# Flamingo block on one core: residual transposed by token tiles inside the last out tile, router ahead of the last routes, six query copies on ScalarE

## The chip, the cores and the metric

One NeuronCore of a Trainium2 chip runs the whole program in one launch. The metric is the device time of the program in microseconds (us), taken as the median of several runs. TensorE (PE in the profile) does matmuls and transposes into PSUM, ScalarE (ACT) and VectorE (DVE) read PSUM and write SBUF, GpSimd (POOL) works on SBUF alone, and SyncE (SP) issues DMAs. Each engine executes its own list of instructions in order and waits on semaphores for the others.

## The reference, cut to what matters

```python
# x: 4 x 1024 x 256, ctx: 4 x 154 x 256, 16 heads of 16
x = x + tanh(g_xattn) * xattn(layernorm(x), ctx, ctx)        # xpos rotation on q and k, softmax over 154 keys
x = x + tanh(g_ffn) * ffn(layernorm(x))

def mole(x, W, b, A, Bm, Rw):                                # three LoRA experts of rank 8
    gates = softmax(x @ Rw)                                  # 3 gates for each token
    z = einsum('bsd,edr->ebsr', x, A)                        # 24 values for each token
    return x @ W + b + 1/8 * einsum('ebsr,erh->bsh', z * gates, Bm)
def ffn(x):
    return mole(relu(mole(x, W1, b1, A1, B1, R1)), W2, b2, A2, B2, R2)     # 256 -> 1024 -> 256
```

## The kernel before, in words

The 4 x 1024 tokens are cut into eight chunks of 512 tokens (c = 0 to 7), each of four token tiles of 128 (k = 0 to 3). The kernel is a pipeline of eight steps written out by hand, one for each chunk, and one epilogue. Step c does the attention of chunk c, the second layernorm, the router and the hidden layer of chunk d = c - 1, and the output layer (the "out tiles") of chunk e = c - 2. So step 0 has attention alone, step 1 ("second") has no out tiles, and steps 2 to 7 ("full") have all three. Each engine has its own function `step` with its own order, and the semaphores (`Count`, with `at(n, k)` for the k-th signal of step n) tie the orders together. Nothing plans the order at build time: it is the order of the lines.

Most matmuls run in fp32r on operands split in a high and a low part: three products instead of one. So each operand on its way from PSUM is copied once (the high part) and subtracted once (the low part).

The stretch that the change touches lies in the middle of a step, in this order on TensorE (its `step` begins at L1178):

- out tile 3 of chunk e (`out_tile(e, 3)`, L1112): 8 hidden tiles x 3 products into bank 0 of `psF`; its last 28 columns are the second router's and the LoRA values (z2).
- `transpose_x(d, ...)` (L943): eight 128 x 128 transposes of the normalised residual `xn` of chunk d into two banks of `psX`, feature half f = 0 first with its four token tiles, then f = 1. It waits until all four tiles of `xn` are written by ScalarE (L411).
- `q_transposes` for g = 0 and 1 (L1085): the rotated queries of chunk c, four transposes for each of eight groups g, into bank g % 4 of `psX`.
- `lora2_operand(e, 1)` (L1122): transposes of the gated LoRA values `zs` of out tiles 2 and 3.
- `router1(d)` (L1028): the first router and LoRA values (z1) of chunk d, which need the high and the low part of the transposed residual (`xT_hi`, `xT_lo`).
- `out_lora(e, 1)` (L1128), then `q_transposes` for g = 2 to 7, with the two halves of the first hidden tile (`hidden_main(d, 0)`, L1052) behind g = 3 and g = 5, and `lora1_operand(d)` (L1037).
- Then a loop of 16 `max_scores` (L1099), each with half a hidden tile; VectorE reduces each one (L733) and writes the low half of each hidden tile (L726).

On ScalarE (`step` at L455) the same stretch is: `normalise` (four tiles of `xn`), the exponential of the second router's gates for tiles 2 and 3 (`gate2_exp(e, 1)`, L440), `x2T_high` (the high part, two copies, L356), then the copies of the queries of g = 0, 2, 4, 6 into `qT` (L356); behind the first of them stand `gate2_copy(e, 1)` and `gate1_exp(d)`.

On VectorE: statistics of the first layernorm of chunk c + 1 (L574, L579), `copy_z2(e, 3)` (L740), `gates2(e, 1)` (L590 to L614: maximum, shift, exponential by ScalarE, sum, reciprocal, weights, gated values, and their split into `zs`), `x2T_low(d)` (the low part, L639), the query copy of g = 1 (L721), `gates1_shift(d)` (L783, L590, L592), g = 3, `gates1_weigh(d)` (L598 to L614), `finish(e, 2)` (L751), g = 5, `finish(e, 3)`, g = 7, and the loop of reductions.

`max_scores(0)` of TensorE waits until six of the eight query groups are copied (L1093 to L1095), three by either engine, and `max_scores(1)` for all.

Of the kernel before, what the change touches and what calls it, by code (L numbers as in the profile page):

```python
# [65 lines left out]
def build(nc, x, ctx_in, wq, wkv, wo, w1, w2, a1, lora, tables, out):  # L66
    with ExitStack() as stack:
# [121 lines left out]
        qT_ps, qT_a, qT_v = count("qT_ps", NG), count("qT_a", NG // 2), count("qT_v", NG // 2)  # L189
# [164 lines left out]
        def _(act):  # L354
# [100 lines left out]
            def step(b, u, first=False, second=False, last=False):  # L455
# [22 lines left out]
                if full:  # L478
                    gate2_exp(e, 1)
# [3 lines left out]
                for g in range(0, NG, 2):  # L483
                    act.wait_ge(qT_ps.sem, qT_ps.at(c, g + 1))
                    copy(qT[0:KS, g, :], psX[0:KS, g % 4, :]).then_inc(qT_a.sem, 1)
                    if full and g == 0:
                        gate2_copy(e, 1)
                    if not first and g == 0:
                        gate1_exp(d)
# [79 lines left out]
        def _(dve):  # L569
# [25 lines left out]
            def gates_weigh(v, e, n, i, K, e_done):  # L595
# [15 lines left out]
                V.tensor_copy(zs[:, K, 0:NL], zg[:, K])  # L611
                V.tensor_copy(zs[:, K, 64:64 + NL], zg[:, K]).then_inc(v.sem, 1)
# [181 lines left out]
            def step(b, u, first=False, second=False, last=False):  # L794
# [31 lines left out]
                if not last and not first:  # L826
                    ln1_stats(c + 1)
                if full:
                    copy_z2(e, 3)
                    gates2(e, 1)  # L830
                if not first:
                    x2T_low(d)
                q_transposed(c, 1)
                if not first:
                    gates1_shift(d)
                q_transposed(c, 3)
# [4 lines left out]
                q_transposed(c, 5)  # L841
                if full:
                    finish(e, u, 3)
                q_transposed(c, 7)
# [86 lines left out]
        def _(pe):  # L931
# [6 lines left out]
            def transpose_x(c, banks, src_s, ps):  # L938

                pe.wait_ge(src_s.sem, src_s.at(c))  # L940
                for f in range(FT):
                    for k in range(TT):
                        ins = nc.tensor.transpose(banks[:, f, tokens(k)], xn[:, k, P * f:P * f + P], ident)  # L943
                    ins.then_inc(ps.sem, 1)

# [126 lines left out]
            def q_transposes(c, g, first):  # L1072

                if g == 0:
                    pe.wait_ge(q_lo.sem, q_lo.at(c))
                    pe.wait_ge(q_hi2.sem, q_hi2.at(c))
                elif g == 2 and not first:
                    pe.wait_ge(x2T_hi_s.sem, x2T_hi_s.at(c - 1))
                    pe.wait_ge(x2T_lo_s.sem, x2T_lo_s.at(c - 1))
                elif g >= 4 and g % 2 == 0:  # L1080
                    pe.wait_ge(qT_a.sem, qT_a.at(c, g // 2 - 1))
                elif g >= 4:
                    pe.wait_ge(qT_v.sem, qT_v.at(c, g // 2 - 1))
                for k in range(TT):
                    ins = nc.tensor.transpose(psX[0:KS, g % 4, tokens(k)].bitcast(F32R), qs[:, k, g, :], ident_r[:, :])  # L1085
                ins.then_inc(qT_ps.sem, 1)

            def max_scores(c, i):
# [3 lines left out]
                if i < 2:  # L1092
                    n = 3 if i == 0 else 4  # L1093
                    pe.wait_ge(qT_a.sem, qT_a.at(c, n))
                    pe.wait_ge(qT_v.sem, qT_v.at(c, n))  # L1095
# [7 lines left out]
            def out_tile(d, k, m0=0, m1=HT):  # L1103
# [4 lines left out]
                if k == 3:  # L1108
# [69 lines left out]
            def step(b, u, first=False, second=False, last=False):  # L1178
# [23 lines left out]
                if full:  # L1202
# [4 lines left out]
                    out_tile(e, 3)  # L1207
                if not first:
                    transpose_x(d, psX[:, 2:4, :], ln2_out, x2T_ps)
# [3 lines left out]
                for g in range(2):  # L1213
# [3 lines left out]
                if not first:  # L1217
                    router1(d, second)
                if full:
                    out_lora(e, 1)  # L1220
                for g in range(2, NG):
                    q_transposes(c, g, first)
                    if not first and g in (3, 5):
                        hidden_main(d, 0, second, (g // 2 - 1,))
# [83 lines left out]
LAST = B * UB - 1  # L1308
F_OF_K = [0, 1, 2, 0]
# [71 lines left out]
```

## Time and profile before

| | us |
|---|---|
| median of 3 runs | 604.42 |
| lowest, highest | 602.23, 604.69 |
| the profiled execution, its own time | 603.83 |
| span of the profiled execution, first to last instruction | 602.0 |
| busy in it: PE, DVE, ACT, POOL | 524.9, 416.3, 238.3, 84.9 |

The time of an execution is 1.8 us longer than the span of its profile. The rows further down are read in a few views: the page (busy times and chain shares), the waits (who waited for whom), the chain of waits (followed back from the last instruction, at each step to what released it), the timeline of one engine, the groups of instructions, and windows (busy times and the granted clock of a stretch). An instruction is named by its line, what it writes and what it reads: `DVE L639 ... xT_lo<-psX,xT_hi` is the low part of the transposed residual. In a timeline `x2` means two instructions merged into one row, and `[0.61 <-DVE zs L614]` that the engine had been idle for 0.61 us until that instruction released it. The full steps repeat one another closely; the step shown is that of c = 5, at 340 to 406 us.

### The profile page before, as it was taken

The numbers are of one execution on the slowest core, as the hardware profiler recorded it, in microseconds if no ns is written. First come the engines' busy times: TensorE is split into PE (matmuls) and PEld (weight loads), VectorE is DVE, ScalarE is ACT, GpSimd is POOL, SyncE is SP. The second block draws the span as 40 slices with busy tenths as digits, with TensorE's granted clock in tenths as the row PEclk, the third lists the DMA queues.
The fourth block names the chain that finished last, engine by engine and source line by source line (L and its number), as shares of the span: only waits on it lengthen the run. The fifth ranks groups of instructions, "written<-read, shape, count | busy, mean of one in ns | idle before, by whom it ended". The sixth has DMA issues, their size and how long they took to land.

```text
span 602.0 us, 8537 instructions
## 1 busy us (share of the span) xinstructions
PE 524.9 (87%) x3360; PEld 400.0 (66%) x3360; DVE 416.3 (69%) x960; ACT 238.3 (40%) x389; POOL 84.9 (14%) x121
## 2 busy tenths in 40 slices
PE   2668864999989998999989998999899999989795
PEld 1545454855977487856976497738885697649574
DVE  4667355867989478958888488867896578644423
ACT  3252514363354624454335424452436343442210
POOL 2426012011110112011201121011201110101000
PEclk9865975999999999999999999999999999999798
DMA  7301010010101000011002010101002000200000
GB/s 265 112 2 36 2 35 2 0 49 1 37 0 44 31 35 2 37 48 35 1 1 73 1 35 1 66 19 36 1 4 70 0 2 1 73 1 1 2 35 36
DMA packets 6132, 18.50 MB, mean 31 GB/s; under 512 B 932, under 2 KB 1772, under 8 KB 5964
## 3 DMA queue, kind: packets, MB, share of 16 engines
q10 hardware_dynamic: 4005, 12.53, 6.0%
q1 hardware_dynamic: 2087, 5.42, 2.7%
q8 instruction: 27, 0.44, 0.3%
q14 instruction: 13, 0.11, 0.1%
HBM read 13.49 MB, written 4.19 MB: 29 GB/s over the span
## 4 chain that ended last, share of the span: by engine, by line
PE 71%; DVE 16%; ACT 8%; issue 3%; POOL 1%; DMA 1%; ACTq 0%; DVEq 0%
PE psF L1112 17%; PE psF L1052 11%; PE psX L1099 6%; ACT probs L521 4%; PE psX L988 4%; PE psX L1158 4%; PE psX L970 4%; DVE max_t L733 4%; PE psO L1172 3%; PE psF L1172 3%; PE psF L1175 3%; PE psO L1175 3%; PE psF L1058 2%; PE psX L1085 2%; DVE h_lo L726 2%
## 5 line engine op out<-in xcount | busy, mean ns | idle before, releaser
L733 DVE TENSOR_REDUCE max_t<-psX 128x4 fp32r<-128x616 f32 x128 | 99.8, 795 | 6.0 <-PE psX L1099 3.0
L521 ACT ACTIVATE probs<-psX 128x1024 f32<-128x1024 f32 x64 | 63.8, 1024 | 50.5 <-PE psX L1158 50.5
L1112 PE MATMUL psF<-w_hi,h_hi 128*128 128x284 f32 x256 | 76.8, 300 | 2.4 <-DVE h_lo L726 1.5
L1112 PE MATMUL psF<-w_lo,h_hi 128*128 128x284 f32 x256 | 75.2, 294 | 0.0
L1112 PE MATMUL psF<-w_hi,h_lo 128*128 128x284 f32 x256 | 74.9, 293 | 0.0
L1099 PE MATMUL psX<-km,qT 96*128 96x308 f32 x256 | 65.2, 341 | 7.1 <-DVE max_t L733 3.6
L1099 PEld LDWEIGHTS psX<-km,qT 96*128 96x128 f32 x256 | 48.7, 204 | 23.8 <-DVE max_t L733 12.1
L431 ACT ACTIVATE h_hi<-psF 128x512 fp32r<-128x512 f32 x64 | 37.3, 594 | 63.0 <-PE psF L1058 63.0
L726 DVE SCALAR_TENSOR_TENSOR h_lo<-psF,h_hi 128x512 fp32r<-128x512 f32 x64 | 43.7, 685 | 15.7 <-ACT h_hi L431 15.7
L1112 PEld LDWEIGHTS psF<-w_hi,h_hi 128*128 128x128 f32 x256 | 48.2, 188 | 7.8 <-issue 4.6
L311 POOL TENSOR_TENSOR x<-x,tab 128x256 f32<-128x256 f32 x32 | 22.3, 730 | 206.3 <-DMA x<-in_x_dram 206.3
L1052 PE MATMUL psF<-xT_lo,w_hi 128*128 128x512 f32 x128 | 51.4, 412 | 0.0
L1158 PE MATMUL psX<-qT,km 98*128 98x512 f32 x128 | 44.8, 445 | 4.3 <-ACT probs L521 4.0
L1112 PEld LDWEIGHTS psF<-w_hi,h_lo 128*128 128x128 f32 x256 | 48.3, 188 | 0.0
L1112 PEld LDWEIGHTS psF<-w_lo,h_hi 128*128 128x128 f32 x256 | 48.2, 188 | 0.0
L1052 PE MATMUL psF<-xT_hi,w_hi 128*128 128x512 f32 x128 | 42.3, 412 | 1.0 <-DVE zc L783 1.0
L1158 PEld LDWEIGHTS psX<-qT,km 98*128 98x128 f32 x128 | 20.5, 195 | 32.3 <-issue 15.5
L1052 PE MATMUL psF<-xT_hi,w_lo 128*128 128x512 f32 x128 | 40.9, 401 | 0.0
L757 DVE STREAM_TRANSPOSE heads_t<-psF 128x512 f32<-128x512 f32 x16 | 11.5, 717 | 34.7 <-PE psF L1175 34.7
L323 POOL TENSOR_TENSOR probs<-probs,tab 128x1024 f32<-128x1024 f32 x8 | 19.0, 2370 | 106.0 <-DVE probs L646 106.0
L1085 PE MATMUL psX<-ident_r,split 128*96 128x128 f32 x256 | 24.7, 250 | 4.9 <-DVE split L678 4.9
L1085 PEld LDWEIGHTS psX<-ident_r,split 128*96 128x96 f32 x256 | 22.9, 133 | 8.1 <-issue 6.0
(155 smaller groups left out, 990.2 us busy)
## 6 DMA issues: line engine op xcount, KB each, us to landing
x<-in_x_dram ACTq DMA_DIRECT2D x8, 512.0 KB, 3.3
x_ln<-in_x_dram ACTq DMA_DIRECT2D x7, 512.0 KB, 3.3
out_dram<-x ACTq DMA_DIRECT2D x7, 512.0 KB, 2.6
heads_t<-in_w_dram SPq DMA_DIRECT2D x1, 1024.0 KB, 8.5
heads_t<-in_w_dram SPq DMA_DIRECT2D x1, 994.0 KB, 4.6
tab<-in_tables_dram SPq DMA_DIRECT2D x1, 674.0 KB, 7.0
x_ln<-in_x_dram SPq DMA_DIRECT2D x1, 512.0 KB, 3.4
wkv_sb<-in_wkv_dram SPq DMA_DIRECT2D x1, 512.0 KB, 9.8
```

The source lines that it names most:

```text
L431: nc.scalar.activation(h_hi[:, m, :], psF[:, (m + 1) % 3, :], ACT.Relu).then_inc(w1_hi_s.sem, 1)
L521: nc.scalar.activation(dst, psX[:, 2 * (i % 2):2 * (i % 2) + 2, :], ACT.Exp).then_inc(sc_exp.sem, 1)
L726: V.scalar_tensor_tensor(out=h_lo[:, m, :], in0=psF[:, (m + 1) % 3, :], scalar=0.0, in1=h_hi[:, m, :].bitcast(F32), op0=ALU.max, op1=ALU.s ...
L733: V.tensor_reduce(max_t[:, k, half, :].rearrange("p (h g) -> p g h", h=2)[:, 2 * j:2 * j + 2, :], psX[:, 2 * j:2 * j + 2, 0:2 * S].rearran ...
L970: ins = mm(o_ps, a[:, f, tokens(k)], w[:, f, :], start=n == 0, stop=n == 5)
L1052: mm(psF[:, (m + 1) % 3, :], w[:, f, P * m:P * m + P], a[:, f, :], start=n == 0, stop=False)
L1085: ins = nc.tensor.transpose(psX[0:KS, g % 4, tokens(k)].bitcast(F32R), qs[:, k, g, :], ident_r[:, :])
L1099: ins = mm(psX[:, g % 4, 0:2 * S], qT[0:KS, g, tokens(k)], km[0:KS, g, :, :].rearrange("p h s -> p (h s)"), start=True, stop=True)
L1112: ins = mm(psF[:, F_OF_K[k], 0:W2N], a[:, m, tokens(k)], w[:, m, :], start=m == 0 and i == 0, stop=m == HT - 1 and i == 2)
L1158: ins = mm(o_ps, km[:, n // 2, j, 0:P], qT[:, n // 2, :], start=True, stop=True)
L1172: mm(pv_bank(g), vr_sb[:, g, :], probs_r[:, g, :], start=True, stop=False)
L1175: ins = mm(pv_bank(g)[32 * j:32 * j + 32, :], v_sb[:, h, :], probs[:, h % 8, :], start=False, stop=True)
```

## The change: what it does

- TensorE's out tile 3 is cut in two: six of its eight hidden tiles (18 matmuls), then the transposes of `xn`, then the last two hidden tiles (6 matmuls). The new `transpose_x2` goes by token tiles: for each k it waits for that tile of `xn` alone and transposes both feature halves.
- `router1(d)` stands directly behind the query groups 0 and 1. Groups 2 to 5 follow, then `lora2_operand(e, 1)`, the first half of hidden tile 0, `out_lora(e, 1)`, groups 6 and 7, the second half of hidden tile 0, `lora1_operand(d)`.
- ScalarE copies the query groups 0, 1, 2, 3, 4, 6 and VectorE 5 and 7 (before: four each). `gate2_exp(e, 1)` moves from ahead of `x2T_high` to behind group 1; `gate2_copy(e, 1)` and `gate1_exp(d)` from behind group 0 to behind group 3.
- VectorE does `x2T_low(d)` ahead of `copy_z2(e, 3)` and `gates2(e, 1)`, and `gates1_shift`, group 5, `gates1_weigh`, `finish(2)`, group 7, `finish(3)` behind them.
- The two copies of the gated values into `zs` (its columns 0 and 64 on) become one instruction with the input read twice.
- The waits follow: a group g of 4 or more waits for copy g - 3 of ScalarE; `max_scores(0)` for five copies of ScalarE and one of VectorE. The epilogue keeps its order, and has the one copy into `zs`.

```diff
@@ -186,7 +186,7 @@
         q_ps, q_evac = count("q_ps", 2), count("q_evac", 2)
         q_cos, q_sin, q_rot = count("q_cos", 1), count("q_sin", TT), count("q_rot", 1)
         q_hi, q_hi2, q_lo = count("q_hi", 1), count("q_hi2", 1), count("q_lo", 1)
-        qT_ps, qT_a, qT_v = count("qT_ps", NG), count("qT_a", NG // 2), count("qT_v", NG // 2)
+        qT_ps, qT_a, qT_v = count("qT_ps", NG), count("qT_a", 6), count("qT_v", 2)
...
@@ -475,17 +475,17 @@
                          q_rc.rearrange("p k (g r) -> p (k g) r", r=32)).then_inc(done.sem, 1)
                 if not first:
                     normalise(1, x1[:, 1 - u], d, ln2_rstd, ln2_out, (xT_ps, c))
-                if full:
-                    gate2_exp(e, 1)
                 if not first:
                     x2T_high(d)
 
-                for g in range(0, NG, 2):
+                for g in QT_ACT:
                     act.wait_ge(qT_ps.sem, qT_ps.at(c, g + 1))
                     copy(qT[0:KS, g, :], psX[0:KS, g % 4, :]).then_inc(qT_a.sem, 1)
-                    if full and g == 0:
+                    if full and g == 1:
+                        gate2_exp(e, 1)
+                    if full and g == 3:
                         gate2_copy(e, 1)
-                    if not first and g == 0:
+                    if not first and g == 3:
                         gate1_exp(d)
                 if not first:
                     gate1_copy(d)
@@ -608,8 +608,8 @@
                                 zw[:, K].unsqueeze(3).to_broadcast([P, nk, NE, R]),
                                 ALU.mult).then_inc(v.sem, 1)
                 dve.wait_ge(v.sem, v.at(n, i + 6))
-                V.tensor_copy(zs[:, K, 0:NL], zg[:, K])
-                V.tensor_copy(zs[:, K, 64:64 + NL], zg[:, K]).then_inc(v.sem, 1)
+                V.tensor_copy(zs[:, K].rearrange("p k (t r) -> p k t r", r=32)[:, :, 0::2, 0:NL],
+                              zg[:, K].unsqueeze(2).to_broadcast([P, nk, 2, NL])).then_inc(v.sem, 1)
                 dve.wait_ge(v.sem, v.at(n, i + 7))
                 V.tensor_tensor(zs[:, K, 32:32 + NL], zg[:, K], zs[:, K, 0:NL].bitcast(F32),
                                 ALU.subtract).then_inc(v.sem, 1)
@@ -825,23 +825,21 @@
                     copy_z2(e, 2)
                 if not last and not first:
                     ln1_stats(c + 1)
+                if not first:
+                    x2T_low(d)
                 if full:
                     copy_z2(e, 3)
                     gates2(e, 1)
                 if not first:
-                    x2T_low(d)
-                q_transposed(c, 1)
-                if not first:
                     gates1_shift(d)
-                q_transposed(c, 3)
+                q_transposed(c, 5)
                 if not first:
                     gates1_weigh(d)
                 if full:
                     finish(e, u, 2)
-                q_transposed(c, 5)
+                q_transposed(c, 7)
                 if full:
                     finish(e, u, 3)
-                q_transposed(c, 7)
                 for i in range(16):
                     reduce_max(c, i)
                     if first and i == 5:
@@ -943,6 +941,15 @@
                         ins = nc.tensor.transpose(banks[:, f, tokens(k)], xn[:, k, P * f:P * f + P], ident)
                     ins.then_inc(ps.sem, 1)
 
+            def transpose_x2(d):
+
+                for k in range(TT):
+                    pe.wait_ge(ln2_out.sem, ln2_out.at(d, k + 1))
+                    for f in range(FT):
+                        ins = nc.tensor.transpose(psX[:, 2 + f, tokens(k)], xn[:, k, P * f:P * f + P], ident)
+                        if k == TT - 1:
+                            ins.then_inc(x2T_ps.sem, 1)
+
             def ctx_transposed(b, src):
 
                 pe.wait_ge(ctx_loaded.sem, ctx_loaded.at(b))
@@ -1077,10 +1084,8 @@
                 elif g == 2 and not first:
                     pe.wait_ge(x2T_hi_s.sem, x2T_hi_s.at(c - 1))
                     pe.wait_ge(x2T_lo_s.sem, x2T_lo_s.at(c - 1))
-                elif g >= 4 and g % 2 == 0:
-                    pe.wait_ge(qT_a.sem, qT_a.at(c, g // 2 - 1))
                 elif g >= 4:
-                    pe.wait_ge(qT_v.sem, qT_v.at(c, g // 2 - 1))
+                    pe.wait_ge(qT_a.sem, qT_a.at(c, g - 3))
                 for k in range(TT):
                     ins = nc.tensor.transpose(psX[0:KS, g % 4, tokens(k)].bitcast(F32R), qs[:, k, g, :], ident_r[:, :])
                 ins.then_inc(qT_ps.sem, 1)
@@ -1090,9 +1095,8 @@
 
                 half, k, j = i // 8, i % 8 // 2, i % 2
                 if i < 2:
-                    n = 3 if i == 0 else 4
-                    pe.wait_ge(qT_a.sem, qT_a.at(c, n))
-                    pe.wait_ge(qT_v.sem, qT_v.at(c, n))
+                    pe.wait_ge(qT_a.sem, qT_a.at(c, 5 + i))
+                    pe.wait_ge(qT_v.sem, qT_v.at(c, 1 + i))
                 else:
                     pe.wait_ge(max_red.sem, max_red.at(c, i - 1))
                 for g in range(4 * half + 2 * j, 4 * half + 2 * j + 2):
@@ -1105,7 +1109,7 @@
                 if k == 0:
                     pe.wait_ge(w1_hi_s.sem, w1_hi_s.at(d))
                     pe.wait_ge(w1_lo_s.sem, w1_lo_s.at(d))
-                if k == 3:
+                if k == 3 and m0 == 0:
                     pe.wait_ge(y_out.sem, y_out.at(d, 1))
                 for m in range(m0, m1):
                     for i, (a, w) in enumerate(((h_hi, w2_hi), (h_lo, w2_hi), (h_hi, w2_lo))):
@@ -1204,24 +1208,30 @@
                     out_tile(e, 2, 0, HT // 2)
                     out_lora(e, 0)
                     out_tile(e, 2, HT // 2, HT)
-                    out_tile(e, 3)
-                if not first:
-                    transpose_x(d, psX[:, 2:4, :], ln2_out, x2T_ps)
+                    out_tile(e, 3, 0, HT - 2)
+                if not first:
+                    transpose_x2(d)
                     pe.wait_ge(x1_s.sem, x1_s.at(d))
                 else:
                     pe.wait_ge(q_evac.sem, q_evac.at(c))
-                for g in range(2):
+                if full:
+                    out_tile(e, 3, HT - 2, HT)
+                q_transposes(c, 0, first)
+                q_transposes(c, 1, first)
+                if not first:
+                    router1(d, second)
+                for g in range(2, 6):
                     q_transposes(c, g, first)
                 if full:
                     lora2_operand(e, 1)
                 if not first:
-                    router1(d, second)
+                    hidden_main(d, 0, second, (0,))
                 if full:
                     out_lora(e, 1)
-                for g in range(2, NG):
-                    q_transposes(c, g, first)
-                    if not first and g in (3, 5):
-                        hidden_main(d, 0, second, (g // 2 - 1,))
+                q_transposes(c, 6, first)
+                q_transposes(c, 7, first)
+                if not first:
+                    hidden_main(d, 0, second, (1,))
                 if not first:
                     lora1_operand(d)
                 for i in range(16):
@@ -1306,6 +1316,7 @@
 PV_AFTER = [3, 5, 8, 10]
 PV_SLOT = {3: 0, 5: 1, 8: 2}
 LAST = B * UB - 1
+QT_ACT = [0, 1, 2, 3, 4, 6]
 F_OF_K = [0, 1, 2, 0]
```

## Rows read from the trace of the kernel before

**Rows 1.** The page, part 1: busy us, share of the span, instructions.
```profile
PE 524.9 (87%) x3360; PEld 400.0 (66%) x3360; DVE 416.3 (69%) x960; ACT 238.3 (40%) x389; POOL 84.9 (14%) x121
```
**Rows 2.** The page, part 4: shares of the chain that ended last.
```profile
PE 71%; DVE 16%; ACT 8%; issue 3%; POOL 1%; DMA 1%; ACTq 0%; DVEq 0%
```
**Rows 3.** Waits of PE, whole span: us in total, times, longest.
```profile
PE psO L1122 <- DVE zs L614: 7.3, 8, 2.3
PE psF L1028 <- DVE xT_lo L639: 6.7, 7, 1.0
PE psX L1099 <- DVE qT L721: 2.7, 6, 0.4
```
**Rows 4.** Chain of waits, 338 to 412 us: start us, us, what.
```profile
357.57 4.72 PE psF L1112 x36
...
364.20 0.10 DVE zs L612
...
364.54 1.21 DVE xT_lo L639 x2
...
365.88 1.08 PE psF L1028 x32
...
371.23 0.52 PE psX L1099 x2
```
**Rows 5.** Timeline of PE, 340 to 384 us: start, us, instruction, idle before.
```profile
362.36 1.09 PE L943 MATMUL psX<-ident_r,xn 128*128 128x128 f32 x8
363.21 0.77 PE L1085 MATMUL psX<-ident_r,split 128*96 128x128 f32 x8
364.59 0.34 PE L1122 MATMUL psO<-ident_r,zs 128*96 128x128 f32 x2 [0.61 <-DVE zs L614]
...
370.34 0.45 PE L1037 MATMUL psO<-ident_r,zs 128*96 128x128 f32 x4
```
**Rows 6.** Timeline of ACT, the same stretch.
```profile
360.23 2.08 ACT L411 ACTIVATE xn<-x,ln_b,ln_r 128x256 f32<-128x256 f32 x4 [2.20 <-POOL ln_b L304]
...
363.05 1.08 ACT L356 ACTIVATE xT_hi<-psX 128x512 fp32r<-128x512 f32 x2
```
**Rows 7.** Timeline of DVE, the same stretch.
```profile
362.32 0.19 DVE L740 COPY zc<-psF 128x28 f32<-128x28 f32 x1 [0.36 <-PE psF L1112]
...
367.02 0.32 DVE L783 STREAM_TRANSPOSE zc<-psF 128x128 f32<-128x128 f32 x1 [0.69 <-PE psF L1028]
...
367.97 0.69 DVE L721 CAST qT<-psX 96x512 fp32r<-96x512 f32 x1 [0.23 <-PE psX L1085]
...
370.01 0.48 DVE L751 SCALAR_TENSOR_TENSOR x<-psF,gate,x 128x256 f32<-128x256 f32 x1
...
371.99 0.79 DVE L733 TENSOR_REDUCE max_t<-psX 128x4 fp32r<-128x616 f32 x1
```
**Rows 8.** Groups by form: count | busy us, mean ns | idle before.
```profile
L721 DVE CAST qT<-psX 96x512 fp32r<-96x512 f32 x32 | 21.8, 680 | 4.6 <-PE psX L1085 4.5
L356 ACT ACTIVATE qT<-psX 96x512 fp32r<-96x512 f32 x32 | 18.8, 589 | 16.4 <-PE psX L1085 16.4
...
L611 DVE CAST zs<-zg 128x96 fp32r<-128x96 f32 x8 | 1.7, 211 | 0.3
```
**Rows 9.** Chain of waits, 75 to 125 us, in step c = 1.
```profile
95.32 2.08 ACT xn L411 x4
97.45 1.97 PE psX L943 x8
...
100.88 1.94 PE psF L1028 x32
```
**Rows 10.** Timeline of ACT, 88 to 112 us.
```profile
99.45 0.60 ACT L356 ACTIVATE xT_hi<-psX 128x512 fp32r<-128x512 f32 x1 [0.26 <-PE psX L943]
```
**Rows 11.** Windows: us, busy of each engine, granted clock, DMA share, GB/s.
```profile
105.20:107.20 2.00, 2.00 (x15) 1.71 (x14) 1.41 (x5) 0.59 (x1) 0.00 (x0) 0.60 0.00 0
...
355.00:371.20 16.20, 14.14 (x143) 12.95 (x143) 14.05 (x51) 8.64 (x17) 3.33 (x8) 1.00 0.01 2
```

## The prediction

> **What bounds the kernel now.** The page first: TensorE is busy for 524.9 of 602.0 us [rows 1], and the chain that ended last runs through it for 71%, through VectorE for 16% and ScalarE for 8% [rows 2]. So a change is worth what it takes out of TensorE's idle time on that chain, not what it takes from another engine. The waits come next. In the stretch that the change touches TensorE waits for three things: for the gated LoRA values ahead of the second LoRA operand, for the low part of the transposed residual ahead of the router, and for the last query copies ahead of the first maxima [rows 3]. Of these totals, six full steps carry 0.61, 0.95 and 0.44 us each in the step shown (the other five within 0.2 us of it), 2.0 us together.
>
> The chain through the step of c = 5 tells why. Out tile 3 ends at 362.29, VectorE then works off the second gates until 364.54, only then the low part of the residual until 365.75, then the router starts at 365.88, and the first maxima at 371.23 [rows 4]. The low part could have been made earlier: its input was transposed by 363.45 and copied by ScalarE by 364.13 [rows 5, 6]. VectorE's order holds it back behind the gates, which nobody needs so early. The granted clock is 1.00 here, the 2.4 GHz level [rows 11], so no part of the wait is a slow array.
>
> **The full step, moment by moment.** I lay the new order over the same step with the old durations.
>
> TensorE. One matmul of the out tile takes 4.72/36 = 0.131 us [rows 4], so the 6 that now stand behind take 0.79, and the first 18 end at 361.50. The tiles of the normalised residual end at about 360.8, 361.3, 361.8 and 362.31 [rows 6]. A transpose starts every (363.21 - 362.36)/8 = 0.106 us and takes 0.27 [rows 5]. Token tiles 0 to 2 are done by 362.13; tile 3 starts at 362.36, as the first transpose did before, and its two halves are readable at 362.63 and 362.74 instead of about 362.95 and 363.37. The 6 matmuls follow until 363.37, the query groups 0 and 1 until 363.9.
>
> ScalarE makes the two high parts until 363.73, 0.4 earlier. Its exponential no longer stands in front, which costs nothing here: the copies had to wait 0.1 us for it.
>
> VectorE is idle from 361.96 [rows 7], so the low parts start at 363.26 and, with 0.60 us from one to the next [rows 4], end at 364.54 instead of 365.75: 1.21 earlier. The router starts at 364.69, which leaves TensorE 0.8 us idle ahead of it.
>
> Behind it VectorE has no gap any more, and its list sets the pace:
> - second gates, from 362.32 to 364.54 before = 2.22 [rows 4, 7], now less one copy. The second copy adds 0.10 [rows 4]; the joint one is wider, of which the nearest row is 96 columns in 211 ns [rows 8]. The ends are 0.10 saved and 0.11 lost; I take 0.07 saved: 2.15, to 366.69;
> - transpose of z1, maximum and shift: 367.02 to 367.97 less 0.23 idle = 0.72 [rows 7], to 367.41;
> - copy of query group 5: 0.61, to 368.02;
> - weights and gated values: 367.97 + 0.61 = 368.58 to 370.01 = 1.43 [rows 7], less 0.07: to 369.38;
> - two finishes and one copy: 370.01 to 371.99 held two of each, 1.98 [rows 7]; less one copy, 1.37: the first reduction can start at 370.75 instead of 371.99.
>
> TensorE beside it: router to the first LoRA operand took 370.34 - 365.88 = 4.46 [rows 4, 5]. The second LoRA operand is new in this stretch, 0.34 at most [rows 5]. So it is ready at 364.69 + 4.8 = 369.5, and VectorE's values are there at 369.38 + 0.09 + 0.13 (as from low part to router) = 369.6. The operand takes 0.45, the first maxima start at 370.05: their wait for copies (0.44) is gone, because all but group 7 are copied by 368.6 on ScalarE and 368.1 on VectorE. That is 371.23 - 370.05 = 1.18 on TensorE and 1.24 on VectorE. I take **1.2 us for each of six full steps, 7.2 us**. The loop behind it, in which both engines keep the same lead, has no deadline that isn't set by this start, so nothing takes it back.
>
> The two more copies on ScalarE (589 ns each against 680 on VectorE [rows 8]) are hidden by its 0.5 to 2.4 us gaps. The exponential is wanted at 364.54 + 0.62 = 365.16 (before, 362.32 to 362.94); ScalarE's group 0 can start at 363.8, group 1 ends at 364.9. So its cover is 0.3 us thick. Behind group 3 the gate copy and the router's exponential end at about 367.8, wanted at 368.0: cover 0.2. If either cover is gone, each 0.1 us late costs 0.1 us in each step.
>
> On VectorE's joint copy the page "VectorE: DVE Perf Modes" of the Trainium skill (Mode 2x_2P) bears: a copy within SBUF moves two elements a cycle when the outermost dimension splits evenly over the two read ports, otherwise one. The input here is read twice through a zero stride and the output strided; if that loses the mode, my estimate from the page's 0.96 GHz is 0.05 and 0.10 us longer, and the sum would be 7.7 instead of 8.3 below. No row shows such a copy.
>
> **The other steps.** In step c = 1 there is no out tile. The residual's last tile ends at 97.40, the eight transposes run 97.45 to 99.42, the second high part ends at 100.05, the router starts at 100.88 [rows 9, 10]. The transposes start every 0.20 us here, at half clock, so with tiles 0 to 2 done beforehand the second half of tile 3 is readable at about 98.2 and its high part ends at 99.1; VectorE's two low parts, 0.60 apart behind 98.6, end at 99.9. The router starts at 100.0: 0.9 us gained. Ends: 0.4, if the clock comes back at the same moment as before and the work pulled ahead of it runs at half rate, and 1.3.
>
> The clock there: it reads 0.60 over 105.2 to 107.2 [rows 11], so it went from 1.2 to 2.4 GHz at about 106.8, some 9 us after TensorE began again at 97.45. "TensorE: Matmul & The Clock Gate" (Part 1) of the Trainium skill says that full rate follows sustained activity; by that rule the transposes that start at 96 would bring it forward by up to 1.5 us, and the sum would be about 0.4 higher.
>
> Step c = 0 has no residual. ScalarE's copies in series still keep ahead of TensorE at half clock: nothing. The epilogue keeps its order; two gate chains lie on its path, 0.07 each, with the first gates 0.2.
>
> **Sum.** 7.2 + 0.9 + 0.2 = 8.3 us. Against the profiled execution's 603.83 that is 595.5; the median of the runs is 0.6 above it, which gives 604.42 - 8.3 = **596.1 us**.
>
> **Rivals.**
> - A, as worked out: 596.1, its own range 594.3 to 597.9 (1.0 to 1.35 a step, 0.4 to 1.3 in step 1). Chance 62%.
> - B, the thin covers and TensorE's turns eat half: semaphores and starts that I put at zero add 0.6 us a step to VectorE's list. Every handoff of the new order has under 0.5 us to spare. 6 x 0.6 + 0.6 = 4.2, so 600.2. For it: no gap is left on the list. Against: the old chain shows only 0.02 to 0.15 us at a handoff. 17%.
> - C, the clock comes back early in step 1: half of the 6 us between 100.9 and 106.8 is up to 3 us more, 593.1. Against: the idle time ahead is shortened by 1.5 of 7.6 us only. 8%.
> - D, no change that can be told: ScalarE serves group 2, group 3 and the gate copy (0.59 + 0.59 + 0.38) only after the router's shift at 367.41, so its exponential comes 1.0 us late. 6 x 0.2 + 1.1 = 2.3, 602.1. For it: groups 2 and 3 are transposed behind the router now. Against: they are there 1 us before the shift ends. 8%.
> - E, slower: ScalarE's strict order. The 6 matmuls (0.79), groups 0 and 1 on TensorE (0.55) and their two copies (1.18) stand ahead of the second gates' exponential. If they run behind the low part instead of beside it, the exponential comes at 364.54 + 2.52 = 367.06, 1.9 late: 6 x 0.7 lost against before, less 1.1 elsewhere, 607.5. It decides from 1.4 us late on. Against: they wait for nothing of VectorE. 5%.
>
> **How the numbers follow.** Three runs of the kernel before lie within 2.5 us, so under 0.5%, 3.0 us, can't be told from no change. Faster by more: A, C and most of B, 85%. Within: D and the rest of B, 10%. Slower: E, 5%. The range goes from C's neighbourhood to B, 592.8 to 600.5; it leaves out D, E and the thin ends, under 2 in 10.
>
> **What would show it.** In a full step: no wait of TensorE for the gated values, about 0.8 us for the low part still, 0.2 or less ahead of the first LoRA operand, none for query copies; VectorE without a gap from the low parts to the first reduction; out tile 3 ending 1.1 us later against the last normalised tile, and the first maxima 7.7 instead of 8.9 us behind that tile. The prediction is wrong if VectorE stands waiting for an exponential, if the low parts don't start within 1.0 us of the last normalised tile, or if the step's 1.2 us come back as waits in the loop of reductions.

## The result and the profile after

The changed kernel takes 590.59 us (median of 4 runs, 589.12 to 592.8) against 604.5 us of the kernel before (median of 4, 602.23 to 604.69). The ratio is 0.978, 95% interval 0.976 to 0.980: 13.9 us faster. In a second comparison it took 592.24 us against 604.1 us, 0.979 (0.977 to 0.981). I had said 596.1, with 592.8 to 600.5: right in sign, too small by 5.5 us, and outside the range.

The page of the changed kernel (profiled execution 589.12 us, span 587.3), parts 1 and 4, to lay beside [rows 1] and [rows 2]:

```profile
PE 519.7 (88%) x3360; PEld 394.4 (67%) x3360; DVE 403.1 (69%) x920; ACT 245.9 (42%) x405; POOL 84.8 (14%) x121
...
PE 68%; DVE 15%; ACT 10%; issue 3%; POOL 3%; DMA 1%; ACTq 0%; DVEq 0%
```

GpSimd's share of the chain rose from 1% to 3% and ScalarE's from 8% to 10%: the chain now runs through the second layernorm. The waits of TensorE, to lay beside [rows 3]:

```profile
PE psF L1035 <- DVE xT_lo L639: 5.0, 7, 1.0
...
PE psO L1126 <- DVE zs L614: 3.6, 2, 2.2
```

The wait for the gated values went from eight times to the two of the epilogue, the wait for query copies is gone, and the one for the low part went from 6.7 to 5.0 us. The chain through the full step c = 5, against [rows 4]:

```profile
348.70 0.29 DVE ln_m L579 x3
...
349.53 1.04 POOL ln_r L301
...
350.96 2.08 ACT xn L411 x4
...
353.09 0.34 PE psX L949
...
353.46 0.61 ACT xT_hi L356
...
354.09 1.30 DVE xT_lo L639 x2
...
355.52 1.08 PE psF L1035 x32
356.60 1.24 PE psX L1090 x16
357.85 0.14 PE psO L1126 x2
...
360.28 0.29 PE psO L1044 x4
360.56 0.35 PE psX L1103 x2
```

Before, the chain came through out tile 3 and the second gates; now it goes from the layernorm's statistics over GpSimd's power to the four normalised tiles, one transpose, the high and the low part, the router, and then down TensorE's own list without a break. Both kernels can be read against the end of the last normalised tile, 362.31 before and 353.04 now (starts as in the engines' timelines; the chain counts a matmul from the end of the one ahead and so shows the LoRA operand and the maxima 0.16 us later):

| behind the last normalised tile | before | forecast | measured |
|---|---|---|---|
| low part ends | 3.44 | 2.23 | 2.34 |
| router starts | 3.57 | 2.38 | 2.48 |
| first LoRA operand starts | 8.03 | 7.29 | 7.08 |
| first maxima start | 8.92 | 7.74 | 7.36 |
| first reduction starts | 9.68 | 8.44 | 8.29 |

So the full step gained 1.56 us where I had put 1.2. The timeline of VectorE in the changed kernel (start, us, instruction, idle before) shows one gap from the low part to the first reduction, the 0.27 us in which ScalarE takes the exponential of the second gates. The kernel before had the same 0.27, and it lies inside the 2.22 us that the forecast took for these gates. The rest of the list is without a gap, as forecast:

```profile
354.09 1.29 DVE L639 TENSOR_TENSOR xT_lo<-psX,xT_hi 128x512 fp32r<-128x512 f32 x2 [1.39 <-ACT xT_hi L356]
355.29 0.18 DVE L740 COPY zc<-psF 128x28 f32<-128x28 f32 x1
...
356.14 0.16 DVE L598 TENSOR_REDUCE zsum<-zex 128x2 f32<-128x6 f32 x1 [0.27 <-ACT zex L440]
...
357.22 0.21 DVE L614 TENSOR_TENSOR zs<-zg,zs 128x48 fp32r<-128x48 f32 x1
357.35 0.31 DVE L783 STREAM_TRANSPOSE zc<-psF 128x128 f32<-128x128 f32 x1
...
357.89 0.17 DVE L592 TENSOR_TENSOR zsh<-zc,zmax 128x12 f32<-128x12 f32 x1
357.98 0.68 DVE L721 CAST qT<-psX 96x512 fp32r<-96x512 f32 x1
...
359.48 0.26 DVE L611 CAST zs<-zg 128x192 fp32r<-128x192 f32 x1
359.77 0.26 DVE L614 TENSOR_TENSOR zs<-zg,zs 128x96 fp32r<-128x96 f32 x1
...
361.33 1.63 DVE L733 TENSOR_REDUCE max_t<-psX 128x4 fp32r<-128x616 f32 x2
```

Over the whole span, by the start of the first maxima of steps 1 and 7: 4.6 us came up to step 1 (107.85 to 103.22), 9.3 in the six full steps, 0.7 behind them, 14.7 together. My terms were 0.9, 7.2 and 0.2.

### The profile page after: what moved, and what is told of

Same layout as the page of the kernel before. It is cut to its first block, busy times and chain, and to the rows that moved or that the text cites. A ratio compares the mean times of both kernels' runs of the same rounds, so it can differ in the third digit from the quotient of the medians.

```text
span 587.3 us, 8513 instructions
## 1 busy us (share of the span) xinstructions
PE 519.7 (88%) x3360; PEld 394.4 (67%) x3360; DVE 403.1 (69%) x920; ACT 245.9 (42%) x405; POOL 84.8 (14%) x121
## 4 chain that ended last, share of the span: by engine, by line
PE 68%; DVE 15%; ACT 10%; issue 3%; POOL 3%; DMA 1%; ACTq 0%; DVEq 0%
PE psF L1059 12%; PE psF L1116 11%; PE psX L1103 6%; ACT probs L521 4%; PE psX L977 4%; PE psX L995 4%; PE psX L1162 4%; DVE max_t L733 4%; PE psO L1176 3%; PE psF L1176 3%; PE psF L1179 3%; PE psO L1179 3%; PE psX L1090 3%; ACT xn L411 3%; DVE ln_s L574 2%
## 5 line engine op out<-in xcount | busy, mean ns | idle before, releaser
L521 ACT ACTIVATE probs<-psX 128x1024 f32<-128x1024 f32 x64 | 63.8, 1024 | 49.5 <-PE psX L1162 49.5
L356 ACT ACTIVATE qT<-psX 96x512 fp32r<-96x512 f32 x48 | 26.5, 591 | 15.7 <-PE psX L1090 15.3
L356 ACT ACTIVATE split<-heads_t 128x512 fp32r<-128x512 f32 x16 | 10.0, 626 | 45.1 <-DVE heads_t L772 45.1
```

The source lines that it names most:

```text
L356: return nc.scalar.activation(out_ap, in_ap, ACT.Copy, **kw)
L521: nc.scalar.activation(dst, psX[:, 2 * (i % 2):2 * (i % 2) + 2, :], ACT.Exp).then_inc(sc_exp.sem, 1)
```

## The experiments

Each kernel was timed against the kernel before on the same chip; the median of that kernel is given where it matters. "A full step" below is the change of the distance from the router of step 2 to that of step 7, over five, against the changed kernel's 63.68 us a step. In what was expected, theory S says that VectorE's order bounds the full step, and theory C that part of the gain hangs on TensorE's clock.

**One part undone at a time, on the changed kernel.** VectorE's order:

```diff
-                if not first:
-                    x2T_low(d)
                 if full:
                     copy_z2(e, 3)
                     gates2(e, 1)
+                if not first:
+                    x2T_low(d)
```


> The changed kernel with VectorE's low part of the residual behind the second gates again, all else kept. Theory S (VectorE's order was the bound of the full step): the gates' exponential stands behind ScalarE's group 1 in this order, so the low part ends about 3.0 us later, 6 x 3.0 = 18 us: about 608, router of c = 5 some 5.5 us behind the last normalised tile. Rival (the gain is TensorE's own: transposes inside the out tile): under 1 us a step, below 597.

619.01 us, ratio 1.025 (1.022 to 1.028), 4.2 us a full step. The chain of this kernel in its step c = 5:

```profile
370.72 1.08 ACT qT L356 x2
371.80 0.10 ACT zex L440
...
373.22 1.21 DVE xT_lo L639 x2
...
374.56 1.93 PE psF L1035 x32
376.50 1.65 PE psX L1090 x16
```

The router starts at 374.56, 5.40 behind the last normalised tile (369.16), as theory S said, held by the exponential behind ScalarE's two query copies. The 11 us beyond the forecast are mostly the clock: after TensorE had waited 3.60 us in front of it, the router took 1.93 us instead of 1.08 and the query transposes 1.65 instead of 1.24. It took 1.45 to 1.94 us in five of the six full steps, and 1.08 in one. So the order alone decides some 3 us a step, and the idle time that it makes costs another 1.2 at 1.2 GHz.

**Token tiles.** The out tile whole, the transposes behind all four tiles:

```diff
-                    out_tile(e, 3, 0, HT - 2)
+                    out_tile(e, 3)
...
-                    transpose_x2(d)
+                    transpose_x(d, psX[:, 2:4, :], ln2_out, x2T_ps)
...
-                if full:
-                    out_tile(e, 3, HT - 2, HT)
```


> The changed kernel with out tile 3 whole and the eight transposes behind all four tiles, feature half first, as before. Theory S: out tile 3 ends before the last normalised tile in any case, and only the first half is readable 0.2 to 0.3 us later: 0.25 x 6 + 0.6 in step 1, about 592.7. Rival (token tiles are a main term): 1.2 a step, 598 or more.

595.4 us (before: 603.87), ratio 0.986 (0.983 to 0.989); 0.35 us a full step, where theory S had put 0.25. The time as a whole is 2.7 us above its 592.7. By its profile this kernel is 5.9 us behind the fastest execution of the changed kernel: 2.8 up to the first maxima of step 1, 2.0 in the six full steps and 1.0 behind the first maxima of step 7. Against the slowest execution of the changed kernel it is 0.65 us ahead up to step 1. So the 2 us of the full steps are the token tiles'; the rest is not shown to be, because the clock moves these two stretches from one execution to the next (below).

**Query copies.** Four on each engine:

```diff
-QT_ACT = [0, 1, 2, 3, 4, 6]
+QT_ACT = [0, 2, 4, 6]
...
                     x2T_low(d)
+                q_transposed(c, 1)
...
                     gates1_shift(d)
+                q_transposed(c, 3)
                 q_transposed(c, 5)
```
ScalarE's gate work moves with its list: `gate2_exp(e, 1)` stands behind group 0 here, and `gate2_copy(e, 1)` and `gate1_exp(d)` behind group 2.

> The changed kernel with four query copies on each engine, ScalarE 0, 2, 4, 6 and VectorE 1, 3, 5, 7. Theory S: VectorE has no gap between the low part and the first reduction, so two more copies of 0.6 us put the first maxima 1.15 us later: 6.9 us, about 597.5. Rival (ScalarE's copies are no part of the gain, TensorE's own work is the bound): 591.

599.23 us (before: 603.87), ratio 0.992 (0.989 to 0.995), 1.2 us a full step: theory S, with its 597.5 missed by 1.7 us. Once VectorE's list has no gap, every copy on it is on the path.

**The joint copy into zs**, made two again:

```diff
-                V.tensor_copy(zs[:, K].rearrange("p k (t r) -> p k t r", r=32)[:, :, 0::2, 0:NL],
-                              zg[:, K].unsqueeze(2).to_broadcast([P, nk, 2, NL])).then_inc(v.sem, 1)
+                V.tensor_copy(zs[:, K, 0:NL], zg[:, K])
+                V.tensor_copy(zs[:, K, 64:64 + NL], zg[:, K]).then_inc(v.sem, 1)
```


> The changed kernel with two copies of the gated values into zs instead of one. Theory S: 0.07 and 0.08 us more on VectorE's list in a full step, of which 0.1 reaches TensorE: 0.7 us, 591.3. Rival: nothing.

593.36 us, ratio 0.981 (0.978 to 0.985), which overlaps the changed kernel's interval, so the times can't tell theory S from its rival; in the trace it is 0.14 us a full step. The groups of the changed kernel give the two forms of the joint copy:

```profile
L611 DVE CAST zs<-zg 128x96 fp32r<-128x96 f32 x16 | 3.4, 210 | 0.6
...
L611 DVE CAST zs<-zg 128x192 fp32r<-128x192 f32 x8 | 2.1, 260 | 0.3
```

96 columns more cost 50 ns, about 1.9 elements a nanosecond. "VectorE: DVE Perf Modes" of the Trainium skill gives this mode two results a cycle (Mode 2x_2P) and VectorE a clock of 0.96 GHz (The TRN2 errata). From these figures I estimate 1.92 elements a nanosecond, and the trace agrees: the fast mode is kept with the input read through a zero stride, and the forecast's lower sum for the other case falls away.

**One part alone, on the kernel before.** The orders without token tiles and with four copies each, and the token tiles without the orders (the edits are the parts of the diff above):

> The kernel before with the new orders alone (low part ahead of the second gates, router ahead of the second LoRA operand, gates' exponential behind ScalarE's first copy), but the whole transposes and four copies on each engine. If the parts add: 1.55 gained in the full step, less 0.3 for the tiles and 1.15 for the copies, 0.1 a step: about 603.5. Rival (the orders are the whole gain): 595.

604.27 us against 603.75, ratio 1.001 (1.000 to 1.002). No change, as the sum of the parts said. The chain shows what took the wait's place, VectorE's list with the copies on it:

```profile
362.80 1.29 DVE xT_lo L639 x2
364.09 0.59 DVE qT L721
...
367.43 1.20 DVE qT L721 x2
...
370.12 0.48 PE psO L1037 x4
370.60 0.35 PE psX L1099 x2
```

> The kernel before with the transposes by token tiles inside out tile 3 alone. The gates of tiles 2 and 3 wait for the out tile, which now ends 1.1 us later, and the low part stands behind them: 0.9 us later in each of six full steps, 0.9 gained in step 1: 608.5. Rival (early transposes help by themselves): 600.

616.47 us, ratio 1.021 (1.019 to 1.023): slower, and by more than I had put. Its chain:

```profile
367.04 0.80 PE psF L1121 x6
...
367.87 0.20 DVE zc L740
...
370.08 1.21 DVE xT_lo L639 x2
...
371.43 1.93 PE psF L1037 x32
```

The six matmuls stand in front of the gates, the gates in front of the low part. TensorE's wait for the gated values grew from 0.61 to 1.77 us, the clock read 0.81 over 368 to 372 and 0.50 over 372 to 376, and the router ran at half rate. So neither half of the change is worth anything alone: they come to 0 and +13 us, and the whole, with the query copies moved as well, to -12 to -14.

**The clock.** First the spread of the changed kernel:

> The changed kernel as it is, for its spread. Theory C (some 3 to 4 us of the gain hang on when the clock returns in step 1 and the epilogue): runs at about 589 and about 592, in step with the mean granted clock of 0.958 and 0.951. Rival: one time, whatever the clock.

Five runs: 589.56 us at a mean granted clock of 0.958, 591.23 at 0.954, 592.24 and 592.98 at 0.951, 593.14 at 0.949. The time follows the clock. The kernel before does so more loosely: of 14 runs in this comparison the fastest, 602.82, had 0.950 and the slowest, 606.24, had 0.942, but at 0.945 alone they go from 603.19 to 605.53. The profiled execution of the changed kernel was one of its fastest. Step 1 in it (first fence) and in the profiled execution of this second comparison (second fence), chains of waits:

```profile
83.74 4.61 PE psX L995 x24
...
98.43 1.08 PE psF L1035 x32
99.51 1.26 PE psX L1090 x16
```
```profile
84.87 5.47 PE psX L995 x24
...
100.43 1.94 PE psF L1035 x32
102.36 1.87 PE psX L1090 x16
```

The same instructions of the same program, at 2.4 GHz in the one and at 1.2 in the other. In the second the first maxima of step 1 come at 106.7, which is 1.1 us before the kernel before's 107.85; in the first at 103.22, 3.5 us earlier still.

Much of that lies ahead of the stretch whose order was changed. The first line of each fence is the output projection of step 1. In the kernel before it is

```profile
84.46 5.45 PE psX L988 x24
```

The last normalised tile of step 1, which follows from it, ends at 97.40 in the kernel before, at 95.85 in the first execution and at 97.84 in the second. Behind that tile the router comes after 3.48 us before, and after 2.58 and 2.59 in the changed kernel: 0.9 us gained in both, as forecast, and this is the order. The first maxima come after 10.45, 7.37 and 8.86 us. So of the 4.6 us of the profiled execution 1.55 came ahead of the tile, where the projection started 0.72 us earlier and took 0.84 less; 0.9 is the order; and 2.2 came behind the router, with the router itself at 2.4 GHz and not at 1.2.

Then the kernel was run with TensorE kept busy, and the kernel before likewise:

```diff
+            def busy(bank, n):
+                for _ in range(n):
+                    mm(bank, ident, wkv_sb[:, 0, :], start=True, stop=True)
...
+                if second:
+                    busy(psX[:, 3, :], 10)
                 if not first:
                     project_out(d, c, second)
+                if second:
+                    busy(psX[:, 3, :], 12)
```


> The kernel before, with 10 dummy matmuls (128x512, f32) into a free PSUM bank ahead of the output projection of step 1 and 12 behind it, so that TensorE does not idle there. Theory C: the clock stays at 2.4 GHz through step 1, which takes 2.6 us from the projection and 3 to 4 from the rest of the step: about 598.5. Rival (the clock is no part of it): 604.5 or later.

> The changed kernel with the same dummy matmuls. Theory C: 1.7 us from the projection and 1 to 2 from the rest, 586 to 587, and every run at one time. The difference to the kernel before with the same dummies is then the order alone: 9.3 for six full steps and 1.5 for step 1, 11 us, instead of 13.9. Rival: 590, difference 14.

607.23 and 597.71 us, where theory C had said 598.5 and 586 to 587: both missed, by 9 and 11 us. The clock read 1.00 all through step 1, but in the changed kernel ten dummies ran 80.04 to 88.89 and outlasted the gap, which ended near 85. The difference of the two is 9.5 us, with the clock lower in one place of a full step in either profile; in the changed kernel that step, step 4, took 4.0 us longer. Fitted to the gaps, 5 and 6 of them:

> The kernel before with the same 5 and 6 dummies. Theory C: 598.5, so 11.3 us above the changed kernel with the same dummies: the part of the gain that is the order's. Rival: the clock of step 1 has no part in the gain, and the difference stays at 13 to 14.

> The changed kernel with 5 and 6 dummy matmuls in the two gaps of step 1; the 10 and 12 before took 0.83 us each, twice what I had put, and so outlasted the gaps by 4 us each. Theory C (clock): they now end inside the gaps, the clock stays at 2.4 GHz, the output projection takes 2.9 instead of 4.6 us, the first maxima of step 1 come at 101 us: 587 in every run. Rival: 590 to 592.

600.1 us (0.995, 0.993 to 0.997) and 588.43 us (0.976, 0.974 to 0.979), 11.7 apart, where theory C had said 11.3. Four of the five runs of the latter lie within 0.3 us (588.24 to 588.55, clock 0.964 or 0.965). The fifth, 592.43, is the profiled one, and it is a miss. The clock read 0.69 over 96 to 100: filling these two gaps does not hold it for certain. And step 2 took 2.7 us longer in it than the same step of the changed kernel. That is another cause, a load of context rows (`x_ln<-in_ctx_dram`) that landed late:

```profile
126.61 0.33 PE L959 MATMUL psF<-ident_r,x_ln 128*128 128x128 f32 x1 [0.94 <-DMA x_ln<-in_ctx_dram]
```

Behind it the clock read 0.57 over 128 to 132. Five of the six profiles of kernels with dummies have such a wait, of 0.83 to 1.24 us; in none of the ten others does a matmul wait for these rows. Three of the five lost the clock behind it, and that step took 2.7 to 4.0 us longer; where the clock held, 1.1 and 1.4 us longer. Whether the dummies make the load late was not tested.

> The same, with 10 more dummies behind the key projection of step 0 and 10 behind its value projection. If the clock then stays up in step 0, where it reads 0.50 from 36 to 60 us, 3 to 6 us less than the kernel filled in step 1 alone; if it falls all the same, the dummies run at half rate and cost 2 to 6 us.

601.85 us (0.995, 0.993 to 0.997). That is 4.1 us more than with the dummies of step 1 alone. The 20 dummies of step 0 kept the clock at 1.00 up to 48 us, and cost more than that gave; my 3 to 6 us less was wrong by their length.

**What is left**, the same order in the epilogue, and with fitted dummies in steps 0 and 1:

```diff
-            out_tile(e, 3)
-            transpose_x(d, psX[:, 2:4, :], ln2_out, x2T_ps)
-            lora2_operand(e, 1)
+            out_tile(e, 3, 0, HT - 2)
+            transpose_x2(d)
+            out_tile(e, 3, HT - 2, HT)
             router1(d)
+            lora2_operand(e, 1)
...
+            x2T_low(d)
             copy_z2(e, 3)
             gates2(e, 1)
-            x2T_low(d)
+            gates1_shift(d)
             finish(e, 0, 2)
             finish(e, 0, 3)
-            gates1_shift(d)
```


> The changed kernel with the change's order in the epilogue too: transposes by token tiles inside its out tile 3, low part ahead of the second gates, router ahead of the second LoRA operand. The low part now ends 545.50 in the profiled execution; with transposes readable about 1.5 us earlier and no gates ahead it ends near 542.5. By the order alone 2.5 to 3 us less: 588 to 589 against the changed kernel's 591 to 592. Rival: the wait moves to the gates (the router's values queue behind the second gates on VectorE) and under 1 us is left.

589.68 us (before: 604.36), ratio 0.975 (0.973 to 0.977), against 0.978 and 0.979 of the changed kernel: 0.9 to 2.6 us between the medians, and the intervals overlap. In the trace the last router starts 55.4 instead of 56.8 us behind the first maxima of step 7, and the first LoRA operand 61.3 instead of 63.8. The router's 1.4 us are the order. Of the 2.6 us at the LoRA operand most is the clock: between the two stand twelve hidden matmuls, in the changed kernel (first), in this one (second), and in the next, which has the same order (third):

```profile
548.22 4.60 PE psF L1059 x12
```
```profile
550.74 2.75 PE psF L1059 x12
```
```profile
545.70 5.07 PE psF L1059 x12
```

These matmuls account for 1.85 us of the 2.6, and 0.7 is left for the order: the wait for the gated values, 0.88 us, now stands behind the router. In the third the router comes after 55.3 us and the LoRA operand after 63.9, so nothing is left of it there. The rival named in advance, that the wait moves to the gates and under 1 us is left, fits the traces better than the 2.5 to 3 us that I had put.

> The same with dummies of fitting number: 5 behind the key projection and 7 behind the value projection of step 0, 5 and 6 in the gaps of step 1. With 20 of them in step 0 the clock stayed at 1.00 from 16 to 50 us, but they outlasted the gaps by 8 us. Theory C: 4 to 5 us less in step 0 and 3 in step 1: 580 to 582, the fastest of all. Rival: the clock falls in the loop of step 0 whatever stood ahead, and the saving is what the transposes and projections ahead of it give, 2 us.

587.38 us, ratio 0.973 (0.972 to 0.975), the fastest median, but not the 580 to 582 of theory C. Windows of this kernel (us, busy of PE, PEld, DVE, ACT, POOL, then the granted clock):

```profile
36.00:40.00 4.00, 3.80 (x35) 2.73 (x33) 1.36 (x3) 3.29 (x7) 0.00 (x0) 1.00 0.00 0
40.00:44.00 4.00, 3.25 (x10) 1.90 (x10) 3.77 (x7) 3.57 (x5) 3.60 (x2) 0.75 0.00 0
44.00:48.00 4.00, 2.41 (x7) 1.59 (x7) 3.82 (x13) 0.00 (x0) 2.06 (x5) 0.50 0.00 0
48.00:52.00 4.00, 3.81 (x15) 2.81 (x14) 3.33 (x5) 2.55 (x5) 3.92 (x3) 0.50 0.40 130
```

The clock falls in step 0's loop of maxima, in which TensorE has no hidden tiles to do and takes turns with VectorE's reductions, as the rival had it. But the rival's 2 us are met by luck. The first scores behind the loop start at 56.6 instead of 58.9 us in the kernel above, and the first maxima of step 1 at 99.70 instead of 106.45: 6.75 us gained, near the 7 to 8 of theory C. Then 1.4 went in step 4, where the context rows landed late (TensorE waited 1.24 us), and 2.8 behind the first maxima of step 7, where the clock read 0.50 and 0.68 over 544 to 552. What is left is 2.6 between the two profiled executions.

## Why the prediction was wrong

The mechanism of the full step was right: the low part ahead of the gates, the router 1.1 us earlier, VectorE without a gap but for the gates' own exponential, the query wait gone, the covers on ScalarE holding. Rivals B, D and E didn't happen: the second gates' exponential started 0.5 us behind the low part, and the gate copy ended before it was wanted. E's mechanism is real all the same: with the low part behind the gates it made the kernel 15 us slower than before.

Two terms of the sum failed: the full step was mis-sized, and the clock of step 1 was put at nothing.

*The full step, 1.2 us.* It measured 1.56. "TensorE beside it" took the whole displayed 0.45 us of the first LoRA operand as the time until the maxima; the chain has 0.29 there (0.28 between the starts), and the rest was the tail of a transpose under the next instruction: 0.17. The second LoRA operand went in at "0.34 at most" where the chain has 0.14. And VectorE's list was added part behind part, each from its first start to its last end. An instruction that needs nothing of the one ahead and waits for nobody starts before that one ends, and the new order has three such places between the parts: the copy at 355.29 where the low part ends at 355.38, the transpose of z1 at 357.35 where the gated values end at 357.43, the query copy at 357.98 where the shift ends at 358.06. So from the low part to the gated values it took 4.65 us, not 4.93. It took both errors: by the forecast's 369.5 and 369.6, with one of the two lists put right the other would still have held the first LoRA operand back. Six times 0.36 is 2.2 us.

*Step 1, 0.9 us, with the ends 0.4 and 1.3.* What the term was made of was right: from the last normalised tile to the router the order gained 0.9 us in both profiled executions. The step that failed is the clock beside it: the forecast let it return at the same moment as before, and put all that comes ahead of that tile at nothing. The profiled execution gained 4.6: 1.55 ahead of that tile, where the change moves only step 0's query copies (and step 0's first maxima came 0.4 us later for it), and 2.2 behind the router. The other execution gained 1.1. I had this as rival C with 8% and as one sentence with 0.4 us. The profile showed the size (half rate up to 106.8), and the three times of the kernel before already spread over 2.5 us; I read them as noise to be told apart from the change.

How much of the clock's part the change itself brings is not shown. The clock was back at about 98 us in one execution of the changed kernel and at about 104 in the other, against 106.8 in the one of the kernel before. By the traces the order gained 9.3 us in the full steps and 0.9 in step 1. With fitted dummies in both kernels the difference is 11.7 us, instead of 13.9 and 11.9 without; in both profiles of these the clock still fell once in step 1. So 10 to 12 us are the order's, and the rest comes and goes with the clock.

The range failed for the same reason twice: its low end took either C or the step's upper end, never both, and left nothing for waits that hid overlap. The remaining 0.7 us of the epilogue against 0.2 is clock too, by the trace: its first twelve hidden matmuls took 4.60 us instead of 5.49. Which side of the low end a run falls on is the clock's chance: the slowest of nine, 593.14, lay inside the range.

The rule of "TensorE: Matmul & The Clock Gate" (Part 1) of the Trainium skill, full rate after sustained activity, did not carry me far. The traces don't agree with it everywhere: over 40 to 60 us of the changed kernel TensorE is busy for 17.76 of 20.00 us and the clock reads 0.50 throughout, and over 48 to 52 us of the window table above for 3.81 of 4.00 us, at 0.50 too.

What stays open: what decides when the clock returns in step 1, and whether the change has a part in it. In three of the profiles with dummies a dip in a full step followed a late load of context rows; for the others no cause is shown. The runs show the price, not the trigger.

## What to carry to other kernels

When an engine's list will have no gap left, add its instructions by their distances in a stretch that runs without waits, not by their displayed durations, and take the next part off that list. Here each 0.6 us copy was worth its full price, while the new orders with the copies and the transposes left as they were gained nothing. Price edits together, since an early transpose without the reordered consumer made this kernel 2% slower. And where a stretch of TensorE runs at half clock, compare runs by their mean granted clock before a few us are put down to the order, and measure from an event behind which the change begins, here the last normalised tile, and not from the start.

## What the runs showed of the hardware

- Of one kernel and one input, the time spread over 3.6 us (589.56 to 593.14), in step with the mean granted clock (0.958 to 0.949).
- Six idle stretches of 3.60 us of TensorE in an otherwise busy step were followed by a router at half rate in whole or in part five times; the 0.7 us waits of the changed kernel's full steps were not.
- TensorE waited 0.83 to 1.24 us for a late load of context rows in five of sixteen profiles, all five with dummy matmuls. Where the clock fell behind it (three of the five), the step took 2.7 to 4.0 us longer, elsewhere 1.1 and 1.4 us.
- The output projection of step 1, the same 24 matmuls, took 4.61 us where the clock read 0.57 over 84 to 88 us, and 5.45 and 5.47 us where it read 0.50; in the full step of c = 5 it took 2.89 us at 1.00.
- A matmul of plain float32, 128x512, is two rows in the trace and took 0.83 us in a series at 2.4 GHz.
